# Five of 26 masked score pieces get their mask from DVE instead of PE

## The reference, cut to what matters

```python
scores = jnp.einsum('bhqd,bhkd->bhqk', qh, kh) / jnp.sqrt(jnp.float32(D_K))
scores = jnp.where(mask == 0, NEG_INF, scores)
attn = jax.nn.softmax(scores, axis=-1)
ctx = jnp.einsum('bhqk,bhkd->bhqd', attn, vh)
```

## Time and profile before

| what | us |
|---|---|
| median of 3 runs | 3175.15 (3171.68 to 3175.83) |
| the profiled execution, its own time | 3167.93 |
| its span | 3165.9 |
| PE busy in the span | 2958.0 (93%) |
| DVE busy | 2265.6 (72%) |
| ACT busy | 1730.3 (55%) |
| mask matmuls, line 524: busy | 359.6 |
| unit instruction of the masked phase, line 655: busy | 550.2 |

### The profile page before, as it was taken

One profiled execution on the slowest core, in us unless ns is written; L12 is line 12 of the kernel. 1 busy time (PEld: TensorE's weight loads), 2 busy tenths in 40 slices (PEclk: granted clock), 3 DMA queues, 4 the chain that ended last, 5 costly groups with the idle time before them and its releaser, 6 DMA issues. The chain is left out here.

```text
span 3165.9 us, 97114 instructions
## 1 busy us (share of the span) xinstructions
PE 2958.0 (93%) x41235; PEld 1694.2 (54%) x41235; DVE 2265.6 (72%) x5676; ACT 1730.3 (55%) x2207; POOL 502.0 (16%) x711
## 2 busy tenths in 40 slices
PE   5999999999999999995999999999999999989994
PEld 2566666545655566552466665563333333366662
DVE  6788888587777777747788886238999999551114
ACT  2366677525556556563377777332777777722220
POOL 0255565020000000000222212202000000001113
PEclk8899999979999999996899999997999999989998
DMA  2333333310001100100311111102012211121112
GB/s 72 115 105 107 109 109 91 115 41 24 23 15 24 25 23 17 29 25 27 102 39 39 39 41 47 63 20 85 24 51 67 59 52 32 36 86 44 45 40 77
DMA packets 129376, 172.62 MB, mean 55 GB/s; under 512 B 45199, under 2 KB 99087, under 8 KB 127343
## 3 DMA queue, kind: packets, MB, share of 16 engines
q1 hardware_dynamic: 112672, 119.09, 13.8%
q0 software_dynamic: 10800, 46.76, 4.6%
q10 hardware_dynamic: 5472, 0.56, 0.1%
HBM read 122.76 MB, written 35.16 MB: 50 GB/s over the span
## 5 line engine op out<-in xcount | busy, mean ns | idle before, releaser
L659 DVE TENSOR_REDUCE mpart<-ps 128x1 f32<-128x512 f32 (+5 forms) x2304 | 1242.7, 587 | 146.3 <-PE ps L492 76.1
L492 PE MATMUL ps<-stack 96*32 96x401 bf16 (+5 forms) x13312 | 1261.3, 354 | 9.7 <-DVE mpart L659 5.1
L516 PE MATMUL ps<-stack 99*32 99x512 bf16 (+3 forms) x11648 | 1135.5, 369 | 40.8 <-ACT xT L426 19.3
L426 ACT ACTIVATE xT<-ps 128x1024 f32<-128x1024 f32 (+3 forms) x800 | 732.0, 938 | 439.8 <-PE ps L516 240.6
L426 ACT ACTIVATE cn<-ps 128x1024 f32<-128x1024 f32 (+4 forms) x800 | 686.2, 870 | 314.8 <-PE ps L516 161.0
L492 PEld LDWEIGHTS ps<-stack 96*32 96x32 bf16 x13312 | 491.0, 96 | 497.8 <-DVE mpart L659 231.8
L655 DVE CUSTOM_DVE_ANT_0 scrap<-ps,arena 128x401 bf16<-128x401 f32 (+1 forms) x1024 | 550.2, 574 | 150.9 <-PE ps L492 126.7
L516 PEld LDWEIGHTS ps<-stack 99*32 99x32 bf16 x11648 | 412.6, 97 | 361.7 <-issue 121.3
L544 PE MATMUL ps<-xT,vall 128*17 128x512 f32 (+4 forms) x3648 | 454.9, 504 | 1.8 <-POOL xT L379 1.0
L544 PE MATMUL ps<-cn,vall 128*17 128x512 f32 (+3 forms) x3392 | 440.8, 495 | 1.7 <-ACT cn L426 0.9
L524 PE MATMUL ps<-arena,big 128*32 128x512 fp8e4 (+1 forms) x3264 | 359.6, 382 | 0.0
(11 more groups left out here) (258 smaller groups left out, 2573.4 us busy)
## 6 DMA issues: line engine op xcount, KB each, us to landing
stack<-q_parts SPq DMA_DIRECT2D x384, 64.0 KB, 2.5
wbuf<-in_mask POOLq DMA_DIRECT2D x16, 800.5 KB, 5.1
stack<-k_parts SPq DMA_DIRECT2D x192, 64.0 KB, 2.6
wbuf<-in_maskT POOLq DMA_DIRECT2D x12, 1024.0 KB, 5.2
arena<-in_moe_w SPq DMA_DIRECT2D x19, 512.0 KB, 4.1
stack<-k_parts SPq DMA_DIRECT2D x192, 50.0 KB, 2.2
stack<-sums_inverse SPq DMA_DIRECT2D x16, 512.0 KB, 6.2
parts<-osb SPq DMA_DIRECT2D x240, 32.0 KB
```

The lines of the kernel that those rows point to most:

```text
L426: nc.scalar.activation(e.prob[tile % P_SLOTS][0:rows, half * HALF + first:(half + 1) * HALF], S_PS(g)[0:rows, first:HALF], ACT.Exp, scale= ...
L492: last = nc.tensor.matmul(bank[quarter(j), 0:w], qs[b][0:KQ, t * P + 32 * j:t * P + 32 * j + 32], ks[b][0:KQ, a:a + w], start=True, stop=n ...
L516: last = nc.tensor.matmul(S_PS(g)[quarter(j), lo:hi], ks[b][0:KM, kt * P + 32 * j:kt * P + 32 * j + 32], qs[b][0:KM, half * HALF + lo:half ...
L659: nc.vector.tensor_reduce(dst, src, AX, ALU.max).then_inc(unit_used, 1)
```

## The change

Of the 26 pieces of a head, n = 5, 9, 13, 17 and 21 are named `by_vector`, in the masked phase alone. PE leaves out their eight mask matmuls. DVE gets an instruction for each, which waits for `s_ready`, reads the piece (128 x 1024) from PSUM and the 0/1 mask from SBUF, and writes the sum in place; ACT then waits for the new semaphore `s_masked`. On DVE this instruction stands ahead of the first unit that PE issues in step n-2, the step in which PE issues scores n. In that step PE takes the product first and then all its units (`middle = 0`).

```diff
+    by_vector = [n for n in range(5, ns - 1, 4)] if masked else []
+    due = {}
+    for h in range(H):
+        for n in by_vector:
+            turned = h + (1 if n - 2 <= turn else 2)
+            due[(turned, before[n - 2]) if turned < H else (H + h, n)] = (h, n)
...
-                        act.wait_ge(s_ready, g + 1)
+                        if n in by_vector:
+                            act.wait_ge(s_masked, h * len(by_vector) + by_vector.index(n) + 1)
+                        else:
+                            act.wait_ge(s_ready, g + 1)
...
+                    added_here = masked and n not in by_vector
...
-                            if masked:
+                            if added_here:
                                 last = nc.tensor.matmul(S_PS(g)[quarter(j), lo:hi], e.big16[0:rows, quarter(j)],
...
-                        middle = -(-len(now) // 2)
+                        middle = 0 if n + 2 in by_vector else -(-len(now) // 2)
...
+                def mask_scores(h, n):
+                    kt, rows, half = slots[n][0:3]
+                    dve.wait_ge(s_ready, h * ns + n + 1)
+                    to_mask = S_PS(h * ns + n)[0:rows]
+                    nc.vector.scalar_tensor_tensor(out=to_mask, in0=e.mask_one[0:rows, kt, half * HALF:(half + 1) * HALF],
+                                                   scalar=MASKED, in1=to_mask, op0=ALU.mult, op1=ALU.add).then_inc(s_masked, 1)
...
                     for u in range(nu):
+                        if (h, u) in due:
+                            mask_scores(*due[h, u])
                         if u < MAX_STEPS:
                             finish_max(h - 1, u)
                         unit(h, u)
...
                 for step in range(MAX_STEPS):
                     finish_max(H - 1, step)
+                for n in by_vector:
+                    if (2 * H - 2, n) in due:
+                        mask_scores(H - 2, n)
+                for n in by_vector[:2]:
+                    mask_scores(H - 1, n)
                 scale(0)
                 nc.vector.tensor_copy(last_row.rearrange("p (j r) -> p j r", j=4), ...
+                for n in by_vector[2:4]:
+                    mask_scores(H - 1, n)
                 invert(1)
+                for n in by_vector[4:]:
+                    mask_scores(H - 1, n)
                 scale(1)
```

More of the change, by code:

```diff
@@ L169, in attention_phase @@
         turned_back, fetched = sem("turned_back"), sem("fetched")
-        ahead_in, mask_in, mask_chain, selected = sem("ahead_in"), sem("mask_in"), sem("mask_chain"), sem("selected")
+        ahead_in, mask_in, mask_chain = sem("ahead_in"), sem("mask_in"), sem("mask_chain")
+        selected = sem("selected") if select else None
+        s_masked = sem("s_masked") if masked else None
         v_weights, v_source, v_bias = value
@@ L517, in scores @@
                                                     qs[b][0:KM, half * HALF + lo:half * HALF + hi],
-                                                    start=True, stop=not (crossed or masked))
+                                                    start=True, stop=not (crossed or added_here))
                         for j in range(groups):
```

## The result

The kernel after the change takes 3182.58 us (median of 13 runs, 3179.86 to 3185.6), the kernel before 3175.15 (13 runs, 3171.22 to 3180.59): ratio 1.0025, 95% interval 1.0017 to 1.0033, some 8 us slower. Forecast were 3191 and slower by 16 us: the sign is right, the size twice too big.

What follows compares the result with a forecast made beforehand. PE was taken as the bound; 35.2 us of its work removed, but stalls outweigh it: net 11.9 + 0.44 + 1.71 + 2.0 = +16 us, so 3191 from the median 3175.15, range 3166 to 3212.

Steps and rivals of the forecast that it cites:

- The bound: Stretch 740 to 1340 us: PE busy 599.02 of 600; a matmul left out gains its time until another engine is late.
- The instruction's price: DVE's new 128 x 1024 mask addition in PSUM: 1.22 us long, 1.14 from start to start.
- The middle pieces: Pieces 9, 13, 17: next scores 3.07 us behind the piece against 2.60 of work; stall 0.47, net +0.03 each.
- Piece 5: Behind three units of step 2: PE's last unit ends 3.39 us behind the piece; stall 0.79, net +0.35.
- Piece 21: Units first of a head, each behind a `finish_max` step: 3.45 us behind the piece; stall 0.85, net +0.41.
- Head 14: Pieces 5 to 17 cost 0.44; piece 21's mask waits behind six `finish_max` steps: stall 2.15, net +1.71 us.
- Head 15: No units: stall 0.84, net +0.40 for each of five pieces, 2.0 us; the moved inversion of sums costs nothing.
- the latencies are each a bit shorter: Rival: every chain 0.15 us shorter takes 11 off, leaving +5 us, 3180; chance 0.18.
- DVE has caught up: Rival: step n-3's units are done by T + 0.24 (T: scores' end), so masks start there; -16 us, 3159; chance 0.15.
- DVE becomes the bound: Rival: adding in place in PSUM runs at half the rate, 86 us more, 3277; chance 0.04.
- the maxima land late: Rival: the maxima's DMAs land late for the next head's scores, 7 us on top, 3198; chance 0.11.
- the clock: Rival: PE, idling some 0.5 us in 7, might lose clock 1.00; no reason seen, given no chance.

Runs made afterwards that it cites:

- mask of 32 columns: The changed kernel with DVE masking only the first 32 of each piece's 1024 columns, the rest left unmasked; ratio 0.9882 against the kernel before.
- the nine halves with the product between: Changed kernel, DVE masking the second bank of odd pieces 5 to 21 (tail by PE), product between units; ratio 0.9920 against the kernel before.
- the run that makes it true: The changed kernel with units issued ahead of the scores in steps 2, 6, 10, 14, 18; 3136.05 us, ratio 0.9949 against the kernel before.

## Why the prediction was right, and where its size was off

- **The bound** held: what PE is spared is gained in full where no one is late (mask of 32 columns, 2.19 of 2.2 us a head).
- **The instruction's price**: taken 1.22, measured 1.224. It takes no longer than the product of two 128 x 1024 tensors (1.229 in the earlier trace rows), so PSUM as source and destination and the fp8 operand add nothing that shows.
- **The middle pieces**: stall 0.47 forecast, 0.45 measured; net +0.03 each against +0.04 for all three.
- **Piece 5**: scores 7 forecast 3.39 behind it, measured 3.37 (918.98 to 922.35), a stall of 0.77 in place of 0.79.
- **Piece 21**: forecast 3.45, measured 3.29 (901.11 to 904.40). This term of the sum was too big, by 0.16 us a head. I had taken 0.15 us for each step of `finish_max` from the rows at 902.52 and 902.67. That reading was wrong: the unit that starts at 902.67 waited for PE, not for the step. PE started it at 902.25, its slot of 0.17 us ended at 902.42, and 0.24 behind that is 902.66. Behind the mask the unit has long been ready, and follows the step in 0.09. The first line is of the kernel before, the others of the kernel after:

```profile
902.25 0.37 PE L492 MATMUL ps<-stack 96*32 96x401 bf16 x4
...
902.93 0.17 DVE L693 SCALAR_TENSOR_TENSOR mrest<-mfin,mneg 128x16 f32<-128x16 f32 x1
903.02 0.57 DVE L668 CUSTOM_DVE_ANT_0 scrap<-ps,arena 128x401 bf16<-128x401 f32 x1
```

- **Head 14**: +1.71 forecast for its piece 21; the scores behind it came 3.10 us late against 1.74 of work, so 1.36 - 0.44 = +0.92. I had misread the row at 1353.52: it is of scores 20. Scores 21 start at 1353.96 and, without their mask, would end at 1354.40. Right by that row it would have been +1.27; the rest is that DVE's steps stood closer behind the piece than in the kernel before.
- **Head 15**: +2.0 forecast, 2.0 measured. `scale(1)` ran from 1401.90 to 1404.26 and the next work of DVE was at 1408.13: covered, as forecast.
- **The sum**: 16 forecast, 11.3 in the scores' stretch of the profile, 8 by the runs. The terms above account for 16 to 12: 14 x 0.24 a head (0.16 of it piece 21) and 0.8 in head 14. The rest, from 11.3 in the scores' stretch to 8 by the runs (interval 5 to 10), I can't place. In other versions the two measures also differ by up to 3 us (for the nine halves with the product between, 28.4 us less in the stretch and 25.7 less between medians).
- **How near the size was**: the rival "the latencies are each a bit shorter" (+5 us, 3180) came nearer to the measured 3182.6 than the forecast of 3191. Its mechanism isn't what the traces show: the chains of pieces 5 to 17 are 0.02 us shorter than forecast, not 0.15. Most of the excess was in two wrong readings of rows, for piece 21 and head 14.
- **The other rivals**: "DVE has caught up" was not what the change does, but its condition was right: the run that makes it true starts the mask 0.22 us behind the piece, and behind the middle pieces the scores start 2.67 behind it, for 2.69 forecast. That this run gained 15.0 us between medians, for 16 forecast, is in part luck. Per head it gained 1.03 and not 1.45 (0.53 went to the row of four units, which the rival hadn't counted), and the last two heads cost 1.9 and not 4. "DVE becomes the bound", "the maxima land late" and the clock played no part: the wait for the maxima's DMA isn't among the waits after, and the clock is 1.00.

## What to carry to other kernels

Before work is moved from a full engine to one with room on average, follow one item through: is the other engine free at the moment the item arrives, and what is queued behind the item on it? Here 1.22 us on an engine with a fifth of its time free cost more than 0.44 us on the full one, since it started 0.6 late and two buffers' worth of other work waited behind it. Shorter portions, or its earlier queue issued sooner, give the gain back, while a longer row of items than there are buffers, or an earlier portion standing ahead of the reordered work, takes some of it away again.

## What the runs showed of the hardware

- DVE adds in place in PSUM no slower than it multiplies two tensors of that size without PSUM (1.229 us): 1.224 us for 128 x 1024 (f32 in PSUM, fp8 in SBUF), 0.691 for 512 columns and 0.191 for 32. From these, 1.04 ns a column and some 0.16 us fixed; the next instruction started 1.13 us behind the start (926.70 to 927.83).
- Where DVE's next instruction is ready, a small one of 16 columns costs 0.09 us, not the 0.17 that its row shows (902.93 to 903.02).
